# Top-32 masks of a sparse attention stage: even items by a comparison with a running sum, odd items as a sign function on another engine

## What is computed

```python
Q = (x_text @ Wq).reshape(Bb, Tt, H, DH)          # H, DH = 4, 32
K = (x_vision @ Wk).reshape(Bb, Gg, H, DH)        # Gg = 1601 keys
scores = jnp.einsum('bthd,bghd->bhtg', Q, K) / np.sqrt(DH).astype(np.float32)
scores = jnp.where(vision_mask[:, None, None, :], scores, -jnp.inf)
topv, topi = jax.lax.top_k(scores, K_TOP)         # K_TOP = 32
probs = jax.nn.softmax(topv, axis=-1)
attn = jnp.zeros_like(scores).at[bi, hi, ti, topi].set(probs)
attn_mean = attn.mean(axis=1)                     # mean over the 4 heads
c_t = jnp.einsum('btg,bgd->btd', attn_mean, V)
```

## Time and profile before

| | us |
|---|---|
| median of 3 runs | 3141.91 (3136.61 to 3142.35) |
| the profiled execution, its own time | 3142.94 |
| its span in the trace | 3141.1 |
| VectorE busy over the whole span | 1522.6 (48%) |
| TensorE busy over the whole span | 2434.6 (78%) |
| ScalarE busy over the whole span | 1423.9 (45%) |
| one top-32 loop, `top_ready` of item 1 to that of item 15 | 113.72, 113.79, 114.03, 114.60 in the four batches |

### The profile page before, as it was taken

One profiled execution on the slowest core, in us unless ns is written; L12 is line 12 of the kernel. 1 busy time (PEld: TensorE's weight loads), 2 busy tenths in 40 slices (PEclk: granted clock), 3 DMA queues, 4 the chain that ended last, 5 costly groups with the idle time before them and its releaser, 6 DMA issues.

```text
span 3141.1 us, 37502 instructions
## 1 busy us (share of the span) xinstructions
PE 2434.6 (78%) x13244; PEld 1462.9 (47%) x13244; DVE 1522.6 (48%) x4241; ACT 1423.9 (45%) x2266; POOL 930.0 (30%) x411
## 2 busy tenths in 40 slices
PE   0466598989973996769798669898668888768888
PEld 0432222322222664446476346476346467356466
DVE  8556011121212111794743795743795643696643
ACT  3033376767760222561264561264561354561354
POOL 1013000100002111570290470191461191370191
PEclk9988798999996998669999669999669999669999
DMA  1045633433242111103021103021103011003021
GB/s 57 0 134 185 145 53 66 60 72 47 46 164 65 46 46 38 34 3 109 21 34 37 34 1 111 21 32 40 34 1 111 21 28 42 30 1 104 0 28 41
DMA packets 176807, 168.39 MB, mean 54 GB/s; under 512 B 84065, under 2 KB 147169, under 8 KB 176577
## 3 DMA queue, kind: packets, MB, share of 16 engines
q1 hardware_dynamic: 169088, 156.36, 19.8%
q0 software_dynamic: 7504, 9.35, 1.6%
HBM read 133.52 MB, written 32.32 MB: 53 GB/s over the span
## 4 chain that ended last, share of the span: by engine, by line
PE 56%; DVE 22%; issue 9%; ACT 7%; DMA 4%; SPq 1%; POOL 1%; DVEq 0%; ACTq 0%; POOLq 0%
PE ps L1660 7%; PE ps L1270 5%; PE ps L1281 5%; PE ps L1645 4%; PE ps L1671 4%; DVE sb_xnT L2267 4%; PE ps L1537 3%; ACT sb_arena L937 3%; PE ps L1438 2%; PE ps L1607 2%; PE ps L1451 2%; PE ps L1505 2%; PE ps L1457 2%; PE ps L1587 2%; PE ps L1596 2%
## 5 line engine op out<-in xcount | busy, mean ns | idle before, releaser
L937 ACT ACTIVATE sb_arena<-ps 128x1024 f32<-128x1024 f32 x416 | 402.7, 1021 | 173.3 <-PE ps L1270 163.3
L2408 DVE TENSOR_REDUCE sb_arena<-ps 128x2 f32<-128x1024 f32 x128 | 156.4, 1224 | 271.3 <-PE ps L1671 270.5
L2267 DVE MAX8 sb_xnT<-sb_arena 128x8 f32<-128x60 f32 (+1 forms) x1728 | 246.0, 203 | 80.1 <-ACT sb_arena L1031 80.1
L1270 PE MATMUL ps<-sb_arena 96*128 96x512 bf16 x832 | 241.4, 397 | 52.8 <-issue 33.9
L1660 PE MATMUL ps<-sb_arena 128*128 128x64 f32 x2048 | 242.3, 272 | 0.0
L826 POOL TENSOR_TENSOR sb_arena<-sb_arena 128x1601 f32<-128x1601 f32 x56 | 175.5, 3133 | 217.2 <-DVE sb_arena L2255 217.2
L1660 PEld LDWEIGHTS ps<-sb_arena 128*128 128x128 f32 x2048 | 238.4, 192 | 0.0
L1281 PE MATMUL ps<-sb_arena 128*32 128x512 f32 x1664 | 227.5, 619 | 1.4 <-ACT sb_arena L937 1.4
L1518 PE MATMUL ps<-sb_arena,sb_ones_col 128*1 128x128 bf16 (+1 forms) x832 | 87.7, 287 | 175.7 <-DVE sb_arena L2297 126.0
L1109 ACT ACTIVATE sb_arena<-ps 128x512 f32<-128x512 f32 x256 | 151.7, 593 | 143.8 <-PE ps L1645 143.8
L763 POOL DMA_INDIRECT taken_rows<-sb_taken,sb_slots x32 | 31.3, 979 | 600.3 <-DVEq L2035 591.7
(11 more groups left out here) (341 smaller groups left out, 4568.9 us busy)
## 6 DMA issues: line engine op xcount, KB each, us to landing
sb_arena<-in_ctxT SPq DMA_DIRECT2D x13, 1601.0 KB, 7.2
sb_arena<-k_spill SPq DMA_DIRECT2D x96, 208.0 KB, 8.3
sb_arena<-in_dft SPq DMA_DIRECT2D x5, 2048.0 KB, 7.6
k_spill<-sb_arena SPq DMA_DIRECT2D x12, 832.0 KB, 5.2
sb_arena<-in_w SPq DMA_DIRECT2D x16, 512.0 KB, 6.4
sb_arena<-in_idft SPq DMA_DIRECT2D x4, 2048.0 KB, 8.6
sb_arena<-in_wf SPq DMA_DIRECT2D x8, 1024.0 KB, 11.8
o_rows<-sb_arena SPq DMA_DIRECT2D x32, 256.0 KB, 2.3
```

What stands on the lines that cost most here:

```text
L937: A(probs0[:, 2 * (m % 4):2 * (m % 4) + 2, :], ps[:, 2 * (m % 2):2 * (m % 2) + 2, :], ACT.Exp).then_inc(pair_probs, 1)
L1270: ins = mm(ps[:, 2 * (m % 2) + i, :], k_stack[0:NSPLIT, h, k * P:(k + 1) * P], q_stack[0:NSPLIT, h, :], start=True, stop=True)
L2267: ins = V.max(cand[:, n % 2, 8 * j:8 * j + 8], s_sb[:, n % 6, c0:c0 + w])
```

## The change

Odd items get their mask from ScalarE: Sign(score - threshold), with the threshold put just under the 32nd largest, so that kept scores give +1 and the others -1. It writes the row sums as well (32 - 1569 = -1537 for a row with 32 kept keys). Even items keep VectorE's comparison, which now writes its row sums through an accumulator too. The count is then one matmul of the 128 row sums with a column of ones, and ScalarE's copy of it changes the sign for odd items; the branch compares with 32 x 128 or 1537 x 128. The minus ones go away after GpSimd's product, because the scaling is now a Relu (for items 14 and 15, a maximum with zero in L2306's successor). VectorE computes the bias for Sign in three operations on one column (L2306 to L2308 of the changed kernel). `settle` and `weight` of an odd item move from the fifth to the seventh step of the next item. ScalarE's sum over the 32 best now stands ahead of the count's copy. Sign is in the activation table that is loaded already: each kernel as built has 49 table loads.

```diff
@@ GpSimd
                     pool.wait_ge(e1_ready, nth(b, e1_ready, n + 1))
+                    if n % 2:
+                        pool.wait_ge(sign_ready, nth(b, sign_ready, n // 2 + 1))
@@ ScalarE, scale_head
-                    A(p if n % H1 else p_mean[:, t % 2, 0:GKEYS], p, ACT.Copy, scale=stat1[:, n % 3, WEIGHT:WEIGHT + 1]).then_inc(p1_scaled, 1)
+                    A(p if n % H1 else p_mean[:, t % 2, 0:GKEYS], p, ACT.Relu, scale=stat1[:, n % 3, WEIGHT:WEIGHT + 1]).then_inc(p1_scaled, 1)
@@ ScalarE, item n, behind the exponential
-                    act.wait_ge(count_done, nth(b, count_done, n + 1))
-                    A(kept_by_col[0:1, :], ps[0:1, 7, 3 * P:4 * P], ACT.Copy, accum_out=kept[0:1, n:n + 1]).then_inc(count_ready, 1)
+                    if n % 2:
+                        if n >= 3:
+                            act.wait_ge(count_done, nth(b, count_done, n - 1))
+                            act.wait_ge(p1_kept, nth(b, p1_kept, n - 1))
+                        A(kept01[:, 1, 0:GKEYS], s_sb[:, n % 6, 0:GKEYS], ACT.Sign, bias=under[:, 2:3], accum_out=kept_by_row[:, 1, :]).then_inc(sign_ready, 1)
                     A(top_e[:, n % 2, :], top[:, n % 2, :], ACT.Exp, bias=bias,
                       accum_out=stat1[:, n % 3, SUM:SUM + 1]).then_inc(sum1_ready, 1)
+                    act.wait_ge(count_done, nth(b, count_done, n + 1))
+                    A(kept[0:1, n:n + 1], ps[0:1, 7, 3 * P:3 * P + 1], ACT.Copy, scale=-1.0 if n % 2 else 1.0).then_inc(count_ready, 1)
@@ TensorE, count(n)
-                    pe.wait_ge(choice_ready, nth(b, choice_ready, n + 1))
+                    if n % 2:
+                        pe.wait_ge(sign_ready, nth(b, sign_ready, n // 2 + 1))
+                    else:
+                        pe.wait_ge(choice_ready, nth(b, choice_ready, n // 2 + 1))
...
-                    for i in range(KCH):
-                        k = -i % KCH
-                        ins = mm(ps[0:1, 7, 3 * P:3 * P + KW[k]], ones_col[:, :], kept01[:, n % 2, k * P:k * P + KW[k]],
-                                 start=(i == 0), stop=(i == KCH - 1))
+                    ins = mm(ps[0:1, 7, 3 * P:3 * P + 1], kept_by_row[:, n % 2, :], ones[:, :], start=True, stop=True)
@@ VectorE, item n
-                        if k == 4 and n >= 1:
+                        if k == (6 if (n - 1) % 2 else 4) and n >= 1:
                             settle(n - 1)
                             weight(n - 1)
...
-                    V.tensor_scalar(st[:, NEG:NEG + 1], eights[:, 0:1], -1.0, None, ALU.mult).then_inc(top_ready, 1)
-                    if n >= 2:
-                        dve.wait_ge(p1_kept, nth(b, p1_kept, n - 1))
-
-                    V.tensor_scalar(kept01[:, n % 2, 0:GKEYS], s, eights[:, TOPK - 1:TOPK], None, ALU.is_ge).then_inc(choice_ready, 1)
+                    least = eights[:, TOPK - 1:TOPK]
+                    if n % 2:
+                        if n >= 3:
+                            dve.wait_ge(sign_ready, nth(b, sign_ready, n // 2))
+                        V.tensor_scalar(st[:, NEG:NEG + 1], eights[:, 0:1], -1.0, None, ALU.mult)
+                        V.tensor_scalar(under[:, 0:1], least, JUST_UNDER - 1.0, 1.0e-30, ALU.mult, ALU.add)
+                        link(V.tensor_scalar(under[:, 1:2], least, -1.0 - JUST_UNDER, None, ALU.mult))
+                        V.tensor_scalar(under[:, 2:3], under[:, 1:2], under[:, 0:1], None, ALU.max).then_inc(top_ready, 1)
+                    else:
+                        V.tensor_scalar(st[:, NEG:NEG + 1], eights[:, 0:1], -1.0, None, ALU.mult).then_inc(top_ready, 1)
+                        if n >= 2:
+                            dve.wait_ge(p1_kept, nth(b, p1_kept, n - 1))
+                            dve.wait_ge(count_done, nth(b, count_done, n - 1))
+
+                        V.tensor_scalar(kept01[:, 0, 0:GKEYS], s, least, 0.0, ALU.is_ge, ALU.add, accum_out=kept_by_row[:, 0, :]).then_inc(choice_ready, 1)
```

More of the change, by code:

```diff
@@ L38 @@
 H1, D1, TOPK = 4, 32, 32
-ALL_DECIDED = int(np.float32(P * TOPK).view(np.int32))
+ALL_DECIDED = [int(np.float32(P * n).view(np.int32)) for n in (TOPK, GKEYS - 2 * TOPK)]
+JUST_UNDER = 2.0 ** -22
 DROPPED = -3.4e38
@@ L134, in program @@
         ones_row = sb("ones_row", [P, P], BF16)
-        ones_col = sb("ones_col", [P, 1], BF16)
         norms = sb("norms", [P, 4])
@@ L246, in program @@
         kept01 = at(o, [2, KS], BF16); o += KS
-        kept_by_col = at(o, [P]); o += P
+        kept_by_row = at(o, [2, 1]); o += 2
+        under = at(o, [3]); o += 3
         probs1 = at(o, [3, KS]); o += 3 * KS
@@ L452, in program @@
         sum1_ready = sem("sum1_ready", 16)
-        choice_ready = sem("choice_ready", 16)
+        choice_ready = sem("choice_ready", 8)
+        sign_ready = sem("sign_ready", 8)
         count_ready = sem("count_ready", 16)
@@ L1724, in setup_program @@
                 link(V.memset(ones_row[:, :], 1.0))
-                link(V.memset(ones_col[:, :], 1.0))
                 link(V.memset(every[:, :], 1.0))
@@ L2233, in settle @@
                     kept_bits = dve.value_load(kept[0:1, n:n + 1].bitcast(I32), min_val=0, max_val=2 ** 31 - 1)
-                    with dve.If(kept_bits != ALL_DECIDED):
+                    with dve.If(kept_bits != ALL_DECIDED[n % 2]):
                         dve.wait_ge(e1_ready, nth(b, e1_ready, n + 1))
@@ L2305, in _ @@
                     dve.wait_ge(e1_ready, nth(b, e1_ready, n + 1))
-                    link(V.scalar_tensor_tensor(s_cut[:, 0:GKEYS], kept01[:, n % 2, 0:GKEYS], stat1[:, n % 3, WEIGHT:WEIGHT + 1],
-                                                probs1[:, n % 3, 0:GKEYS], ALU.mult, ALU.mult))
+                    link(V.scalar_tensor_tensor(s_cut[:, 0:GKEYS], kept01[:, n % 2, 0:GKEYS], 0.0, probs1[:, n % 3, 0:GKEYS], ALU.max, ALU.mult))
                     dve.wait_ge(p1_added, nth(b, p1_added, n - TILES))
-                    V.tensor_tensor(mean, mean, s_cut[:, 0:GKEYS], ALU.add).then_inc(p1_added, 1)
+                    V.scalar_tensor_tensor(mean, s_cut[:, 0:GKEYS], stat1[:, n % 3, WEIGHT:WEIGHT + 1], mean, ALU.mult, ALU.add).then_inc(p1_added, 1)
                 dve.wait_ge(p1_added, nth(b, p1_added, TILES * (H1 - 1)))
```

## The result

The changed kernel takes 3154.63 us (median of 6 runs, 3150.26 to 3161.31), where the kernel before takes 3141.14 in the same rounds (6 runs, 3136.61 to 3142.35): a ratio of **1.0048**, 95% interval 1.0035 to 1.0061. It is slower by some 15 us, where 3125 and a gain were forecast. Its profiled execution, the slowest of the six (3161.31), has a span of 3159.5 us (before: 3141.1).

What follows compares the result with a forecast made beforehand. Bound: VectorE's own work and, once per tile, the ring count, context, scores, score copy, search. Per batch 4.8 - 3.2 + 2.0 + 1.0 - 0.3 = 4.3 us, 17.2 in four: 3125 us, range 3105 to 3143.

Steps and rivals of the forecast that it cites:

- T(1) to T(15): One batch's loop; T(n) starts the operation releasing item n's exponential; forecast near 110.5 us instead of 113.7.
- odd count behind E: TensorE's count of an odd item starts 3.3 us after E, the start of that item's exponential on ScalarE.
- ordinary pair: T(n) to T(n+2) for odd items 1, 3, 5, 9: 14.9 us, with VectorE waiting 0.65 for scores.
- pair of item 7, of item 11: Context items, T(n) to T(n+2): 18.6 us against 17.31 and 19.5 against 17.59; 3.2 lost per batch.
- items 13 to 15: Loop end with no scores left to wait for: 12.3 us against 14.36, 2.0 saved per batch.
- last context behind T(15): Tail: last context starts at T(15) + 3.6 us, before 5.22; less 0.6 for the clock, 1.0 saved.
- item 0 to item 1, lost: Start: item 0's comparison is covered by a wait for scores, item 1 has extra operations; 0.3 us lost per batch.
- even comparison: VectorE's comparison with accumulator goes from 2.08 to 1.85 us and waits for nobody; bounds 1.05 and 2.15.
- the mask is not taken as decided: Sign's sums miss -1537 even with 32 kept; slow branch for 32 odd items, some 640 us slower; chance 0.03.
- VectorE all the way: Score ring stays hidden behind VectorE, pairs take 14.2 us, context items unchanged; 11.0 us saved per batch, 3098; chance 0.12.
- The ring takes it all: Items 7 and 11, late exponential through Sign, count, context, scores to search: 5 us lost each, 3152 us; chance 0.13.
- The wait moves: Items 3 and 5 get exponentials 1 us late, clock takes 1 us per context item; 3141 us; chance 0.15.

Runs made afterwards that it cites:

- experiment 2: Changed kernel with Sign's threshold 2^-23 instead of 2^-22 under the 32nd score; 3130.97 us, ratio 0.9988 against the kernel before.
- experiments 1 and 2: 1: changed kernel with the slow branch never taken, 3131.19 us, ratio 0.9989; 2: changed kernel with threshold 2^-23, 3130.97 us, ratio 0.9988.
- experiment 3: Changed kernel with threshold 2^-23, and Sign placed ahead of the exponential on ScalarE; 3094.56 us, ratio 0.9874 against the kernel before.

## Why the prediction was wrong

**The loops: right in their sum, at the context items by luck.** T(1) to T(15) was forecast at 110.5 and measured at 110.88, 110.35 and 110.28, and in the fourth batch at 110.3 without the branch. Terms of the first batch, forecast and measured:

| term, us | forecast | measured |
|---|---|---|
| odd count behind E | 3.3 | 3.33 (item 7) |
| ordinary pair | 14.9 | 15.17, 15.33, 14.97, 14.97 |
| pair of item 7, of item 11 | 18.6, 19.5 | 19.14, 19.15 |
| item 7: count behind T, count to landed scores, from there to T(9) | 4.0, 8.3, 6.3 | 4.74, 8.35, 6.04 |
| the same in the second and third batch | | 3.59, 9.42, 6.05 and 3.59, 9.05, 6.05 |
| items 13 to 15 | 12.3 | 12.15 |
| last context behind T(15) | 3.6 | 3.70 |
| item 0 to item 1, lost | 0.3 | 0.41 |
| even comparison | 1.85 | 1.874 |

In the second and third batch E(7) and E(11) stood at T + 0.25 and not at T + 0.7 and T + 1.6, and the array needed up to 1.1 us more for context and scores than the 8.3 of the sum. The two errors cancel to within 0.6 us in each pair of item 7. VectorE's new wait in ordinary pairs, forecast at 0.65, is 0.58 us at the top of item 3:

```profile
1307.75 0.47 DVE L2275 MAX8 sb_xnT<-sb_arena 128x8 f32<-128x60 f32 x3 [0.58 <-ACT sb_arena L1035]
```

**The slow branch: the step that failed.** The rival "the mask is not taken as decided" had the mechanism and nearly its price (eleven passes and 20 us per item; measured ten passes and 18.4). What failed was its condition: it was put as all 32 odd items or none, and given 0.03 because sums of ones are exact. The exactness of the sum was never in doubt; the threshold was. It lies a fixed fraction under the 32nd score, so it admits any 33rd score in the gap, and the program has 2048 x 4 rows of 1601 scores, half of them on odd items. One row is enough to send its whole item through ten passes. The chance had to be asked of the data, per row, and one such item (18.4 us) already outweighs the whole summed gain (17.2).

The data can be asked: the reference with its own inputs, computed in fp32 on an ordinary processor (so its last bits are not the chip's), gives the distance from the 32nd to the 33rd score of every row. The closest of all 8192 rows is token 49 of head 3 in the fourth batch, at 1.6 x 2^-22 of the score; that row belongs to item 3 of the fourth batch, the one item that took the branch. The next row follows at 9.9 x 2^-22. 140 rows of odd items lie within 2^-12, which gives 0.14 rows within 2^-22: an estimate. By it the branch had a chance of some 13%, not 3%, and that it was taken at all was bad luck as well.

**Unchanged code: the term that was not in the sum.** Without the branch 4 us are left of the 17.2. In the stage that the sum was about, the forecast held: from T(0) to the filters experiment 2 is 15.7 to 17.9 us shorter than before. Against the first trace of before the loops gave 14.3 us (forecast 14.4), the ends of the loops 2.7 (forecast 4.0), and the start took 1.4 (forecast 1.2). What took it back is the code that no edit touches: 1277.1 to 1277.8 us behind the changed kernel and experiments 1 and 2, 1266.9 and 1267.4 before. The sum put that at nothing without a reason. 10.2 us there and 18.4 in the branch are 28.6 of the 29.6 us between the forecast, 3125, and the measured 3154.6.

Of those 10.2 us 5.9 stand in the **last stretch**, from the last batch's filters to the end (288.7 before, 294.6 after, 295.1 in experiment 2), and 3.4 between the first batch's filters and the second T(0). Stretches of before, and at the same distance from the filters in experiment 2:

```profile
2892.47:2912.47 20.00, 16.83 (x56) 9.76 (x55) 7.75 (x17) 6.83 (x11) 0.00 (x0) 1.00 0.00 1
2852.47:3141.10 288.63, 249.35 (x1472) 178.21 (x1472) 148.51 (x212) 115.18 (x246) 99.38 (x45) 0.95 0.19 47
```

```profile
2879.71:2899.71 20.00, 16.82 (x49) 9.53 (x48) 7.75 (x17) 5.71 (x9) 0.00 (x0) 0.83 0.00 0
2839.71:3134.80 295.09, 254.17 (x1472) 181.30 (x1472) 148.10 (x212) 115.19 (x246) 99.25 (x45) 0.93 0.20 46
```

The matmuls are the same 1472, their busy time grows by 4.8 us, and the granted clock in the stretch falls from 0.95 to 0.93. From 40 to 60 us in, it is 1.00 (2.4 GHz) before and 0.83 here, with 49 matmuls in 20 us against 56. Matmul for matmul, experiment 2 is 2.9 us late from 55 us in on and 3.8 late from 151 us in on. Then 1.6 us come from elsewhere: the array waits longer for a DMA, and the last 1.0 us falls into the matmuls behind that wait.

```profile
3125.80 0.37 PE L1688 MATMUL ps<-sb_xtn,sb_arena 128*64 128x64 f32 x1 [8.81 <-DMA sb_arena<-o_rows]
```

```profile
3118.48 0.37 PE L1697 MATMUL ps<-sb_xtn,sb_arena 128*64 128x64 f32 x1 [10.43 <-DMA sb_arena<-o_rows]
```

The last batch of before is a short one at the first of these places: the first matmul of L1612 stood 66.4 to 66.7 us behind the filters in its first three batches and 63.8 in the last, where it stands at 66.5 in the last batch of the changed kernel, in both traces (65.2 in its second and third). Every other kernel of this study took 290.2 to 295.1 us in the last stretch. What decides where the clock falls in unchanged code, and why the DMA came later, was not tried and stays open.

*The rivals.* "VectorE all the way" is refuted by the steps of 8.85 and by experiment 3. "The ring takes it all" is refuted as well: a context pair took 19.15 us, 1.55 to 1.85 over before, under its limit of 3.7. "The wait moves" named 3141 by late exponentials in items 3 and 5; E - T is 0.25 there. The time without the branch, 3131, lies between it and the forecast, by another way.

*What stayed hidden, as said:* Sign's 1.6 us on ScalarE, the later release of GpSimd for odd items, and VectorE's work on items 14 and 15, though here one size was off: L2324 was to take 1.83 us and took 3.3 for item 14, as the last section shows.

## What to carry to other kernels

A decision that was made by an exact comparison and is made anew against a threshold with a margin must be priced by its data: how many rows there are, how likely a neighbour is in the margin, and what one exception costs; here 0.14 rows in 4096 and 18.4 us. Unchanged code behind a changed stage needs a margin of its own, here 14 us between kernels, and two traces of each kernel to see it. When work moves to another engine, place the step that feeds the ring ahead of the steps that nobody waits for: the same Sign two queue places earlier turned a gain of 0.1% into 1.3%, and a context that waits for nothing in front of the count made it 1.8%. Test the cheap half of a change by itself; here the sums and the single matmul gave 0.8% alone, with no second engine, against 0.1% for the whole without its slow branch.
